# A two-layer cross-attention kernel: first layer cut into pieces of a batch, one transpose for the maxima of a whole batch, and a new order on every engine

## The reference

```python
x = x + xattn0(layernorm(x), ctx)     # 16 heads of 8; softmax over 256 context tokens
x = x + butterfly_ffn(layernorm(x))   # 128 -> 512 -> gelu -> 512 -> 128
x = x + xattn1(layernorm(x), ctx, ctx)
x = x + moe_ffn(layernorm(x))         # 16 experts, 4 per token, plus a shared expert

q, k, v = heads(x1 @ Wq + bq), heads(x2 @ Wk + bk), heads(x2 @ Wv + bv)
attn = softmax(q @ k.T / sqrt(8))
out = (attn @ v) @ Wo + bo
```

## Time and profile before

| | us |
|---|---|
| median of 3 runs (217.97 to 218.35) | 218.0 |
| profiled execution, its own time | 219.55 |
| its span | 217.7 |
| PE busy | 206.1 |
| DVE busy | 165.7 |
| ACT busy | 143.2 |
| POOL busy | 47.8 |

### The profile page before, as it was taken

The page is one execution under the profiler, slowest core; times in us unless marked ns, Lnnn a source line. Parts: engine busy times, 40 slices in busy tenths (PEclk is TensorE's granted clock), DMA queues, the critical chain, the costliest instruction groups (busy, mean ns, idle before and its releaser), DMA issues.

```text
span 217.7 us, 3841 instructions
## 1 busy us (share of the span) xinstructions
PE 206.1 (95%) x1528; PEld 112.6 (52%) x1535; DVE 165.7 (76%) x267; ACT 143.2 (66%) x235; POOL 47.8 (22%) x67
## 2 busy tenths in 40 slices
PE   7988999998989999999999999999999999999994
PEld 2344455666654654433435555554576555674641
DVE  0169999889997832566989989899988685886682
ACT  2365566795986899739448789896989967531220
POOL 7968910000285060492000000120000000000000
PEclk9999999999999999999999999999999999999999
DMA  5930000000000036000000000000000000001001
GB/s 173 385 138 0 0 3 0 5 0 5 0 3 0 0 113 230 2 0 0 3 0 0 3 3 0 5 0 0 3 2 3 0 0 0 0 3 48 0 2 48
DMA packets 2658, 6.41 MB, mean 29 GB/s; under 512 B 528, under 2 KB 1088, under 8 KB 2512
## 3 DMA queue, kind: packets, MB, share of 16 engines
q0 software_dynamic: 912, 3.70, 4.7%
q1 hardware_dynamic: 1152, 1.87, 2.4%
q10 hardware_dynamic: 576, 0.60, 0.9%
HBM read 5.64 MB, written 0.52 MB: 28 GB/s over the span
## 4 chain that ended last, share of the span: by engine, by line
PE 81%; DVE 9%; ACT 6%; issue 2%; DVEq 0%
PE PS L316 61%; PE OB L316 20%; ACT P L780 4%; DVE T L912 3%; DVE K L866 1%; DVE Q L870 1%; ACT Q L753 1%; ACT sq L757 1%; DVE x L946 1%; DVE xn L896 1%; DVE Q L918 1%; DVE xn L902 0%; DVE attn L939 0%; DVE x L953 0%; DVE x L1045 0%
## 5 line engine op out<-in xcount | busy, mean ns | idle before, releaser
L780 ACT ACTIVATE P<-PS 128x512 f32<-128x512 f32 x128 | 68.0, 601 | 18.6 <-PE PS L316 18.1
L912 DVE TENSOR_REDUCE T<-PS 128x4 fp32r<-128x1024 f32 x64 | 75.8, 1219 | 5.2 <-PE PS L316 4.4
L316 PE MATMUL OB<-P,V 128*32 128x256 f32 x512 | 33.8, 385 | 0.0
L316 PE MATMUL PS<-K,Q 32*128 32x256 f32 x256 | 29.1, 323 | 0.7
L316 PE MATMUL PS<-Q,K 32*128 32x256 f32 x256 | 27.2, 321 | 1.6 <-ACT P L780 0.9
L316 PEld LDWEIGHTS PS<-K,Q 32*128 32x128 f32 x256 | 17.9, 183 | 16.4 <-DVE T L912 5.3
L697 POOL TENSOR_TENSOR attn<-o_raw,sums 128x512 f32<-128x512 f32 x4 | 5.1, 1276 | 82.4 <-ACT sums L799 82.4
L833 ACT ACTIVATE gate_t<-PS 128x512 f32<-128x512 f32 (+1 forms) x18 | 10.3, 595 | 18.8 <-DVE prod_t L1029 10.9
L316 PEld LDWEIGHTS PS<-Q,K 32*128 32x128 f32 x256 | 17.1, 183 | 9.5 <-ACT P L780 4.2
L316 PEld LDWEIGHTS OB<-P,V 128*32 128x32 f32 x512 | 13.6, 109 | 11.2 <-issue 2.2
L316 PE MATMUL PS<-idle 128*128 128x512 bf16 x48 | 15.7, 455 | 1.9 <-DVE idle L1047 1.2
(11 more groups left out here) (133 smaller groups left out, 302.5 us busy)
## 6 DMA issues: line engine op xcount, KB each, us to landing
w_gu<-gu POOLq DMA_DIRECT2D x1, 1024.0 KB, 5.2
x<-xT SPq DMA_DIRECT2D x2, 256.0 KB, 5.2
cx<-ctxT SPq DMA_DIRECT2D x2, 256.0 KB, 5.3
w<-w2p POOLq DMA_DIRECT2D x1, 512.0 KB, 5.9
outT<-x SPq DMA_DIRECT2D x2, 256.0 KB, 2.0
e_up<-eup POOLq DMA_DIRECT2D x1, 508.0 KB, 5.6
e_dn<-edn POOLq DMA_DIRECT2D x1, 508.0 KB, 5.8
w_exp<-wexp POOLq DMA_DIRECT2D x1, 258.0 KB, 5.8
```

Of the source, the lines that this page charges most:

```text
L316: return nc.tensor.matmul(out, lhsT, rhs, start=start, stop=stop)
L780: finish(nc.scalar.activation(P[:, (JOINT * U + j) % (JOINT * PUNITS), :, :].rearrange("p k q -> p (k q)"), PS[:, FILLED["sc", U, j // 2][ ...
L912: finish(nc.vector.tensor_reduce(dst, two("max", U, i).rearrange("p j (t s) -> p j t s", t=2), AX.X, ALU.max, negate=True), "red", U, i)
```

## The change

- **Pieces.** `SPANS` cuts layer 0 into tokens 0 to 256, 256 to 512 and 512 to 1024, layer 1 into the two chunks as before. `centre` to `normed`, `kproj`, `qproj` and the steps behind them are done for each piece, so there are nine norms instead of eight. The keys of layer 1 are projected in two pieces too. The loads of `x` and `cx` follow the pieces; the identity and layer 1's weights are loaded later, on SP's queue; `selc` is loaded from ACT's queue.
- **Stacks by group.** `ksel` and `qsel` take one group instead of two: two matmuls (high, low) on the same 32 rows into one bank. There are 40 such steps instead of 16 of four matmuls, and 40 evictions of 128x256 or 128x512 elements instead of 16 of 128x1024.
- **Maxima of a batch together.** `red` writes the maxima of group g to column g of each 32 columns of `T` (before always to column 0), and `K` of group g holds its ones on row g. One `turn` serves all units of `TURN_UNITS`: two and two for the first batch, then four. `shift` adds one transposed tile to the queries of all its groups, 128x4x256 elements. There are 9 turns and 9 shifts instead of 32 of each. A `sc` step waits for the shift of its whole batch.
- **New order tables** for all engines.

```diff
+SPANS = (((0, 256), (256, 512), (512, 1024)), ((0, 512), (512, 1024)))
+NORMS = [(s, *span) for s in range(4) for span in SPANS[min(s, 1)]]
+TURNED = ((2, 2),) + ((4,),) * 7
...
 PE_ORDER = """
-fill.17:0 centre.0:0 fill.2:1 avg.0:1 kproj.0:23 vproj.0:45 qproj.0.0:6 fill.2:0 ksel.0.0.0:01 ksel.0.1.0:23
+fill.18:0 centre.0:0 kproj.0.0:1 avg.0:2 fill.1:3 kproj.0.1:3 centre.1:4 qproj.0.0:5 avg.1:6 kproj.0.2:1
...
             def stack(kind, l, p, g):
-                for part, t in enumerate((q_hi, q_lo) if kind == 0 else (k_hi, k_lo)):
-                    for gg in range(2):
-                        rows = slice(32 * (2 * h + gg), 32 * (2 * h + gg) + 32)
-                        last = mm(two(*sel_step)[:, gg, :], selr[rows, 2 * kind + part, :],
-                                  t[rows, chunk(c) if kind else slice(0, CH)],
-                                  start=part == 0, stop=part == 1)
+                rows = slice(32 * g, 32 * g + 32)
+                for part, t in enumerate((q_hi, q_lo) if kind == 0 else (k_hi, k_lo)):
+                    at = lo % CH if kind == 0 else lo
+                    last = mm(bank(*sel_step)[:, 0:hi - lo], selr[rows, 2 * kind + part, :], t[rows, at:at + hi - lo],
+                              start=part == 0, stop=part == 1)
...
-            def turn(U):
-                take()
-                for i in (1, 0):
-                    after(pe, "red", U, i)
+            def turn(t):
+                take()
+                for U in reversed(TURN_UNITS[t]):
+                    for i in (1, 0):
+                        after(pe, "red", U, i)
                 for qt in range(2):
-                    last = mm(bank("turn", U)[:, qt * D:(qt + 1) * D], T[:, U % TURNS, qt, :], selr[:, 4, :])
+                    last = mm(bank("turn", t)[:, qt * D:(qt + 1) * D], T[:, t % TURNS, qt, :], selr[:, 4, :])
...
             def scores(U, i):
-                after(pe, "shift", U)
+                after(pe, "shift", turned_with(U))
...
-            def shift(U):
+            def shift(t):
-                l, b, g = unit(U)
-                filled(dve, "turn", U)
-                finish(nc.vector.tensor_tensor(Q[:, g, queries(b)], bank("turn", U)[:, 0:SEQ],
-                                               Q[:, g, queries(b)].bitcast(f32), ALU.add), "shift", U)
+                l, b, g = unit(TURN_UNITS[t][0])
+                n = len(TURN_UNITS[t])
+                dst = Q[:, g:g + n, queries(b)]
+                filled(dve, "turn", t)
+                finish(nc.vector.tensor_tensor(dst, bank("turn", t)[:, 0:SEQ].unsqueeze(1).broadcast_to([D, n, SEQ]),
+                                               dst.bitcast(f32), ALU.add), "shift", t)
```

More of the change, by code:

```diff
@@ L170, in nth, with columns, pieces, norm @@
     return [s for s in order if s[0] == step[0]].index(step) + 1
+def columns(l, p):
+    return slice(*SPANS[l][p])
+def pieces(l, lo, hi):
+    return [p for p, (a, b) in enumerate(SPANS[l]) if a < hi and b > lo]
+def norm(s, p):
+    return NORMS.index((s, *SPANS[min(s, 1)][p]))
+def turned_with(U):
+    return next(i for i, units in enumerate(TURN_UNITS) if U in units)
 def build_program(nc, xT, ctxT, wqk, wv, woq, cols, selc, mix, bv, gate_b, wexp, wcon, eup, edn, gu, gus, w2p, w2s,
@@ L342, in centre @@
                 else:
-                    after(pe, *(("resid", 0, c), ("ffnadd", c), ("resid", 1, c))[s - 1])
-                give(mm(bank("centre", n), CENTRE, x[:, chunk(c)]), "centre", n)
+                    c = lo // CH
+                    after(pe, *(("resid", 0, c), ("ffnadd", c), ("resid", 1, c))[stage - 1])
+                give(mm(bank("centre", n)[:, 0:hi - lo], CENTRE, x[:, lo:hi]), "centre", n)
             def average(n):
+                stage, lo, hi = NORMS[n]
                 take()
@@ L485, in up @@
                 take()
-                after(pe, "normed", NCH + c)
+                after(pe, "normed", norm(1, c))
                 after(pe, "fwr", 3)
@@ L502, in router_logits @@
                     pe.wait_ge(moe_in, 7 * 16)
-                after(pe, "normed", 3 * NCH + c)
+                after(pe, "normed", norm(3, c))
                 for t in range(4):
```

368 lines of the change are left out of this document (200 added, 168 removed).

## The result

| | before | after |
|---|---|---|
| median of the runs, us | 217.99 (217.96 to 218.35) | 220.81 (220.37 to 225.98) |
| profiled execution, its own time | 219.55 | 220.37 |
| its span | 217.7 | 218.6 |

The ratio is 1.0119, with an interval of 1.0095 to 1.0143: 1.2% slower. I had forecast 212.6 us, in a range of 206.5 to 219.0. Of the four runs of the changed kernel one took 225.98 us with a granted clock of 0.967; it is left out of the ratio.

What follows compares the result with a forecast made beforehand. PE's own list was taken as the bound, 90% or more of every stage. From the profiled span, 217.7 - 3.5 + 7.4 - 8.0 - 4.7 + 3.4 = 212.3 us, with 0.3 for the median 212.6, range 206.5 to 219.0.

Steps and rivals of the forecast that it cites:

- Start: Up to layer 0's first maxima: smaller pieces bring them from 19.30 to 15.8 us, -3.5 us.
- Layer 0's attention: First maxima to last PV of layer 0: from 66.1 to 73.5 us, +7.4, including 5.1 us of waits.
- Row-tiled steps and stacks by group: PE's list: new stacks cost 0.25 or 0.12 us each, +0.4 in all; score and maxima steps left alone +2.1.
- my fourth rival: The case Stacks at their high end: each new stack at full length, +7.2 us, 219.8 us, chance 0.08.
- Turns: PE's list over the whole program: 23 of 32 turns go, 23 x 0.37 = 8.5 us off.
- Work moved into layer 0: Layer 1's keys and other steps enter layer 0's attention; two evictions, 2.46 us, leave the chain between the layers.
- Between the layers: Last PV of layer 0 to first scores of layer 1: from 30.7 to 22.7 us, -8.0.
- Layer 1: First scores to last PV of layer 1: DVE decides by batches, from 54.5 to 49.8 us, -4.7.
- Tail: After layer 1's last PV: five products come in, 5 x 0.68, +3.4 us on 47.1, PE without a gap.
- Waits shrink too: Both attention stages: fewer turns and shifts may halve the waits, 6 us less, 206.6 us, chance 0.20.
- Batches uncovered: Batch boundaries: scores wait for the whole batch's shift, some 2.2 us each, 219.2 us from three on, chance 0.13.
- Stacks at their high end: Stacks by group: each new stack costs both matmuls at full length, +7.2 us, 219.8 us, chance 0.08.

Runs made afterwards that it cites:

- e5: The kernel before, unchanged, run again for a second profile: 218.8 us, span 216.3.
- e15: The kernel before with layer 0's exponentials over 128 of 512 elements (from the fourth unit on) and its reductions over 256 of 1024: 214.76 us.
- e13: The changed kernel with layer 0's exponentials over 128 of 512 elements (from the fourth unit on) and its reductions over 256 of 1024: 231.95 us.
- e1: The changed kernel with the low matmul of every stack left out: 219.93 us.
- e6: The kernel before with the four matmuls of each stack issued group by group: 218.77 us.
- e4: The kernel before without its 32 turns and 32 shifts: 215.17 us.
- e10: The kernel before without layer 1's keys; layer 1's attention reads layer 0's keys: 217.82 us.
- e9: The changed kernel without layer 1's keys; layer 1's attention reads layer 0's keys: 224.98 us.
- e14: The changed kernel with layer 0's exponentials and reductions shortened as in e13, and also without layer 1's keys: 218.18 us.
- e3: The changed kernel without its 9 turns and 9 shifts: 223.9 us.
- e8: The changed kernel with the same steps in the same order, banks given out anew (the one longest free): 257.94 us.
- e16: The kernel before without the 34 idle matmuls behind the first maxima: 229.36 us.
- e2: The kernel before with the low half of every stack left out: 218.58 us.

## Why the prediction was wrong, by its steps

**Start, right.** First maxima at 14.48, 3.4 earlier than in the second profile of before; I had said 15.8, measured from a start that was 1.4 long. The pieces begin earlier than I had them (ACT's timeline of after; in the earlier trace rows the first square is at 8.90):

```profile
7.64 0.39 ACT L815 ACTIVATE sq<-PS 128x256 f32<-128x256 f32 x1 [3.25 <-PE PS L361]
```

First reduction at 15.03 (said 16.3) and first exponential at 31.20 (said near 32): right in kind.

**Evictions and shifts, right.** The same columns as the earlier trace rows:

```profile
L987 DVE TENSOR_TENSOR Q<-PS,Q 128x1024 fp32r<-128x1024 f32 x7 | 8.5, 1220 | 1.7 <-PE PS L361 1.4
L805 ACT ACTIVATE K<-PS,col 128x512 fp32r<-128x512 f32 x9 | 6.0, 690 | 1.5 <-PE PS L361 1.4
L987 DVE TENSOR_TENSOR Q<-PS,Q 128x512 fp32r<-128x512 f32 x2 | 1.4, 681 | 0.0
```

1.22 and 0.68 for the shifts (I took 1.2 and 0.7), 0.69 for an eviction (0.6 to 0.7).

**Layer 0's attention, term by term.** The terms of the sum can be held against TensorE's timeline, start to start, waits included (my sums over e5 and the changed kernel, us):

| TensorE in layer 0's attention | before | after | change | predicted |
|---|---|---|---|---|
| row-tiled steps | 22.7 | 31.0 | +8.3 | +4.8 |
| turns (16, then 5) | 6.4 | 2.2 | -4.2 | -4.1 |
| idle matmuls | 6.0 | 3.1 | -2.9 | -1.3 |
| all other steps | 31.0 | 41.0 | +10.0 | +8.7 |
| waits, a term of their own in the prediction | | | | -0.7 |
| sum | 66.1 | 77.3 | +11.2 | +7.4 |

The miss of 3.8 us is in the row-tiled steps, 3.5; the other rows and the waits nearly cancel. I had said that I was wrong outside 70 to 77; it is 77.3.

**Row-tiled steps and stacks by group, wrong in size: the step that failed.** I gave a stack of one group 0.25 us (512 columns) or 0.12 (256), and the row-tiled steps of layer 0's stage +4.8 us in all. They grew by 8.3. It is not waiting for VectorE and ScalarE: with both relieved they take 20.9 us before (e15) and about 28.9 after (19.8 in e13 from the first PV on, 9.1 ahead of it in the changed kernel), so again 8 us more. The prices read above are 0.23 to 0.68 for a stack of 512 columns where I took 0.25, and 0.34 to 0.43 for one of 256 where I took 0.12, and the stage has 28 stacks of one group where it had 5 of two. My argument "beside a step on other rows the second half can hide" fails beside a single maxima step, where the second matmul is the whole 0.22 (e1); beside two steps it nearly hides, but there the first one costs: it stands alone at the head (0.34), or the two steps no longer run side by side (in e1 the maxima start at 51.45 and the scores at 51.87). What counts is that a stack is now a step of its own, and there are more of them. This is my fourth rival in its place, with another mechanism: I had it as both matmuls at full length. How the 8.3 us divide between the stacks and the score and maxima steps left alone (+2.1 in my sum for the whole program) isn't shown: no run has the changed kernel with stacks of two groups. The rule of the Trainium skill (TensorEngine Tiling (Array Packing), Theoretical Speedup) had pointed the right way, and e6 shows how far it goes: with both groups in one step the order of the matmuls is free (218.77 for 218.54 us).

**Turns, right as a term of the list.** "23 x 0.37 = 8.5 us off PE's list" came out: 4.2 us less in layer 0's stage, 3.6 in layer 1's, 0.4 between. What I took for granted is that slots taken off the list shorten the stage. In the kernel before they did so for less than a third: e4 took out all 32, 11.8 us of slots, and won 3.6; the waits that the profile shows in TensorE's list in layer 0's stage rose from 2.9 to 4.6 us. By that rate 23 turns would be worth 2.6 us and not 8.5. Whether it holds for the changed kernel isn't shown: its profile has TensorE busy for 75.6 of the 77.3 us, so the freed slots were filled, by the row-tiled steps above all. Two of my sums were also rounded too far: the parts named for TensorE's whole list (-8.5, +0.4, +2.1, -0.9) give -6.9 and not "about 6", which makes the second way to the forecast 211 and not 212, and "90% or more of every stage" is 89% in layer 1 and 88% in the tail.

**Work moved into layer 0, wrong in what it frees.** The keys cost 1.3 us between the layers (e10) and at most 2.4 in layer 0's attention (e9; in e14 on top of e13 2.1 in the compared stretch). The prediction said that two evictions of 2.46 us stood in the chain; without them, and without the projection and the stacks, the stage is 1.3 shorter, and TensorE is still busy for 26.6 of its 29.4 us, so that its own list follows close behind. So this move gained nothing and may have lost up to 1 us, and layer 0's own waits (estimated at 5.1 us) had little room for it: in the stretch from the first PV only 2.1 us of waiting were left (e13).

**Between the layers, nearly right.** The first reduction comes 10.4 us after the last PV (10.3 said, maxima). The eight reductions then wait for TensorE four times, 1.4 us in all; two of the rows, on DVE:

```profile
106.69 1.23 DVE L978 TENSOR_REDUCE T<-PS 128x4 fp32r<-128x1024 f32 x1 [0.31 <-PE PS L361]
...
110.00 3.49 DVE L978 TENSOR_REDUCE T<-PS 128x4 fp32r<-128x1024 f32 x3 [0.60 <-PE PS L361]
```

13.6 us to the first scores in place of 12.4, which is the miss of 1.3.

**Layer 1, partly open.** -2.6 in place of -4.7. By the same sums the row-tiled steps grew by 1.2 (1.2 said), the turns gave 3.6 (4.1 said), the idle matmuls with the waits ahead of the next step grew by 2.1 (1.3 said), and all other steps shrank by 2.4 (2.4 said). The waits that I had shrinking by 0.7 did not: what the profile shows of them in TensorE's list rose from 0.8 to 2.1 us. Whether VectorE's batches make them, as I wrote, wasn't tried: no run shortened its reductions there.

**Tail, right.** +3.8 for +3.4. "Without a gap" was wrong at the very end, where the last products wait for `prod` and `hid`; from the chain that ended last (start, us, what):

```profile
211.75 0.70 DVE prod_t L1098
212.47 0.70 DVE hid_t L1108
213.22 2.19 PE OB L361 x4
```

**The rivals.** "Waits shrink too": they did in layer 0, and didn't pay. "Batches uncovered" (the slower case, 219.2): excluded by e3, in which no score waits for a shift and the stages are as long: 77.2 us, and in layer 1 53.0, of which 3.4 us at half clock can account for at most 1.7 (51.9 in the changed kernel). "Stacks at their high end" (219.8) came nearest, and I gave it 0.08; its sign, 0.45 for a stack beside score steps, is met beside two steps and not beside one (0.23 to 0.36). The timeline of before had no step of one group, so 0.25 was the middle between two bounds and not a reading, and "hides like a score step" was the only ground for its low half.

**The clock.** "Should stay 1.00" held in the profile, but not in all executions (0.967 in one; 0.99 in the profile of e3 and 0.98 in that of e9).

## What to carry to other kernels

A slot in the timeline of the busiest engine is what an added step costs, and the most that a removed one can give. Where three engines interlock, take one step out in a trial before counting on it: here 32 turns gave 30% of their slots, 19 idle matmuls nothing that could be measured. When a sum misses, sort the timeline of the busiest engine by the terms of the sum first: here it points at the term that was mis-sized, which no trial isolated. Price a small step by how often it starts, not by its work: a stack of two groups beside a step took no longer than one of a single group. And keep an order and its buffer numbers together; one without the other is another program.

## What the runs showed of the hardware that I had not expected

- The same instructions in the same order with other PSUM banks: 257.94 us for 220.81 (e8). Part of it is the clock, 51.2 us at 0.50 where the changed kernel has none; even with all of that taken off (25.6 us at most) e8's span stays 9.6 us longer, more than any stage of this change moved but layer 0's attention.
- Leaving work out can cost time through the granted clock. e13 and e16 do less than the kernels they come from and took 226.1 and 226.4 us at the least, for 220.4 and 218.0, with stretches of up to 13.7 us at 0.50. In e16 a stretch with TensorE busy for 61% went before. e3 and e9 have such stretches too (3.4 and 6.8 us), and no time that is clearly longer. e2, e4, e10 and e15 also do less and have none before their last 2 us.
- A stack of one group (two matmuls of 32 rows, 512 columns) takes 0.66 us on its own and 0.65 beside a maxima step; a stack of two groups (four matmuls) takes 0.66 beside a score step (e15), and 0.47 where another stack follows.
